# Linear attention, two layer norms and a gated MLP on 8 cores: the output projection in one sweep over eight PSUM banks, and the next tile's attention steps moved

## The reference

```python
qkv = x @ w_qkv; q, k, v = split(qkv, 3)          # 16 heads of 64
q, k = elu(q) + 1, elu(k) + 1
kv = k * v
run_*[t] = d * run_*[t-1] + (kv or k)[t]          # two decays d per head: f and s
out_f = q * run_kv_f / max(sum(q * run_ks_f), 1e-6)   # the same for s
x1 = layernorm(x + concat(out_f, out_s) @ w_out)  # w_out: 2048 x 1024
h  = silu(x1 @ wg.T / 127) * (x1 @ wu.T / 127)    # 3072 wide
y  = layernorm(x1 + h @ wd.T / 127)
```

## Time and profile before

| what | value |
|---|---|
| median of 2 runs | 2699.64 us (2673.45 and 2725.84) |
| profiled execution, device time | 2680.23 us |
| its span, slowest core (core 1) | 2678.6 us; the eight cores 2644.9 to 2678.6 |
| mean granted TensorE clock, core 1 | 0.861 of full speed |
| TensorE busy | 66% of the span |
| VectorE, ScalarE, GpSimd busy | 31%, 20%, 14% |
| chain that ended last | PE 48%, DVE 14%, ACT 13%, DMA 7% |

### The profile page before, as it was taken

How to read it: one execution, slowest core, us unless ns; L and a number is a source line. 1 busy time by engine, 2 the same in 40 slices (tenths; PEclk the granted TensorE clock), 3 DMA queues, 4 the chain that set the end, 5 groups by cost and what they waited for, 6 DMA issues and landing times.

```text
span 2678.6 us, 21229 instructions; the slowest of 8 cores (2644.9 to 2678.6 us)
## 1 busy us (share of the span) xinstructions
PE 1765.9 (66%) x7298; PEld 731.0 (27%) x7298; DVE 832.5 (31%) x994; ACT 537.6 (20%) x574; POOL 384.5 (14%) x308
## 2 busy tenths in 40 slices
PE   0222236788667875777687865877677865787686
PEld 0000012333223322333233322333233322332232
DVE  0122213342234233433334224333334223433111
ACT  0011101230222212221122113221123123221111
POOL 6411111111011111111012011111112001111000
PEclk9666657999879988999889987998799988998898
DMA  9999996324743256324823265313833254314433
GB/s 118 125 124 124 123 129 166 102 83 95 172 123 103 65 140 173 102 67 95 224 87 114 64 150 152 101 53 111 207 102 99 85 163 130 111 59 130 130 106 114
DMA packets 259467, 316.06 MB, mean 118 GB/s; under 512 B 91171, under 2 KB 173092, under 8 KB 257060
## 3 DMA queue, kind: packets, MB, share of 16 engines
q1 hardware_dynamic: 175396, 235.00, 30.7%
q0 software_dynamic: 7168, 46.15, 13.1%
q10 hardware_dynamic: 76800, 33.57, 6.1%
HBM read 318.80 MB, written 54.53 MB: 139 GB/s over the span
## 4 chain that ended last, share of the span: by engine, by line
PE 48%; DVE 14%; ACT 13%; DMA 7%; issue 6%; another core or an unknown queue 5%; POOL 4%; ACTq 1%; DVEq 0%; SPq 0%; POOLq 0%
PE C_ps L719 11%; PE D_ps L719 9%; PE A_ps L391 7%; DVE runs L529 7%; PE C_ps L603 3%; DMA wo_buf<-wo_s 3%; PE C_ps L771 3%; PE D_ps L771 3%; PE D_ps L603 3%; PE A_ps L771 3%; PE B_ps L771 3%; ACT sgb L729 3%; DVE denc L426 2%; DMA wq_buf<-wq_s 2%
## 5 line engine op out<-in xcount | busy, mean ns | idle before, releaser
L719 PE MATMUL C_ps<-y1T,wg_buf 128*128 128x512 bf16 x1536 | 390.5, 413 | 283.7 <-ACT sgb L729 130.1
L391 PE MATMUL A_ps<-xT,wq_buf 128*128 128x512 bf16 x1024 | 280.5, 436 | 170.0 <-DMA wq_buf<-wq_s 136.2
L551 POOL TENSOR_TENSOR runs<-qb,runs 128x1024 f32<-128x1024 f32 x64 | 148.7, 2344 | 1539.1 <-DVE states_sb L538 1539.1
L719 PE MATMUL D_ps<-y1T,wu_buf 128*128 128x512 bf16 x1536 | 347.1, 379 | 1.4 <-DVE hbuf L736 0.4
L736 DVE TENSOR_TENSOR hbuf<-D_ps,sgb 128x1024 bf16<-128x1024 f32 x96 | 117.6, 1225 | 582.2 <-ACT sgb L729 582.2
L719 PEld LDWEIGHTS C_ps<-y1T,wg_buf 128*128 128x128 bf16 x1536 | 155.4, 104 | 515.4 <-issue 377.1
L603 PE MATMUL C_ps<-wo_buf,concat 128*128 128x512 bf16 x512 | 171.0, 419 | 125.0 <-DVE concat L445 62.0
L729 ACT ACTIVATE sgb<-C_ps,cv_sb 128x1024 bf16<-128x1024 f32 x96 | 107.0, 1114 | 522.2 <-PE D_ps L719 433.5
L391 PEld LDWEIGHTS A_ps<-xT,wq_buf 128*128 128x128 bf16 x1024 | 110.3, 110 | 342.0 <-issue 262.3
L719 PEld LDWEIGHTS D_ps<-y1T,wu_buf 128*128 128x128 bf16 x1536 | 149.4, 98 | 185.5 <-issue 7.0
L420 PE MATMUL B_ps<-denr,bones_sb 128*128 128x512 bf16 x128 | 51.3, 493 | 224.1 <-POOL denr L408 180.9
(11 more groups left out here) (71 smaller groups left out, 1242.3 us busy)
## 6 DMA issues: line engine op xcount, KB each, us to landing
wq_buf<-wq_s SPq DMA_DIRECT2D x192, 256.0 KB, 3.8
wg_buf<-wg_s SPq DMA_DIRECT2D x192, 256.0 KB, 3.0
wu_buf<-wu_s SPq DMA_DIRECT2D x192, 256.0 KB, 4.3
wd_buf<-wd_s SPq DMA_DIRECT2D x384, 128.0 KB, 2.3
wo_buf<-wo_s SPq DMA_DIRECT2D x256, 128.0 KB, 3.2
out<-work ACTq DMA_DIRECT2D x64, 256.0 KB, 6.1
xbf<-x POOLq DMA_DIRECT2D x32, 256.0 KB, 187.2
xbm<-xbf POOLq DMA_DIRECT2D x32, 256.0 KB, 4.6
```

The costliest lines, as they stand in the source:

```text
L391: t.matmul(o, a, b, start=f1, stop=f2),
L551: lambda v, q_=qv, r_=kvpart: v.tensor_tensor(r_.rearrange("p (o t) -> p o t", o=2), q_, r_.rearrange("p (o t) -> p o t", o=2), OP.mult),
L719: t.matmul(o, a, b, start=f1, stop=f2),
```

## The change

1. The output projection runs once over `kt`, with `h2` inside it: 8 matmuls a step, into all four PSUM tensors (`bank = (C_ps, D_ps, A_ps, B_ps)`, one per 128 tokens). Its first matmul waits for A_ps and B_ps too. The 6 slots of `wo_buf` hold 3 steps of two halves. All eight evictions come behind the last matmul, in the order c = 2, 3, 0, 1, so that A_ps and B_ps come free first.
2. LN1 is done in two groups of two 128-token blocks, (2, 3) and then (0, 1): sums, two Squares, Ln, Exp, two normalisations, two transposing DMAs.
3. The pieces of the next front move: S2 and S3 both stand behind LN1 and ahead of gate/up (S3 stood behind step 1); S4 to S8 stand behind steps 1, 3, 5, 7, 9; S9 stands between gate/up and down (it stood behind down). The calls inside down are gone.

```diff
-        for h2 in range(2):
-            pspair = (C_ps, D_ps)
-            for k in range(min(6, NKT)):
-                stream_half(sg, "wo", ..., k, h2, k)
-            for kt in range(NKT):
...
-                    if kt == 0 and c == 0:
-                        w = w + (firstB[0] if h2 == 0
-                                 else [(ch_v, ch_v.n)])
+        firstB = [(ch_v, concat_val)] + [
+            (chof(t), v) for key in ("A", "B", "C", "D") for t, v in gPS[key]]
+        bank = (C_ps, D_ps, A_ps, B_ps)
+        for k in range(3):
+            for h2 in range(2):
+                stream_half(sg, "wo", ..., k, h2, k * 2 + h2)
+        for kt in range(NKT):
+            for h2 in range(2):
+                ridx = (kt * 2 + h2) % 6
                 for c in range(NCH):
...
+                        lambda t, o=bank[c][:, h2 * 512:(h2 + 1) * 512],
...
+            if kt + 3 < NKT:
+                for h2 in range(2):
+                    stream_half(sg, "wo", ..., kt + 3, h2, (kt + 3) * 2 + h2)
+        m_wave = ch_m.n
+        for c in (2, 3, 0, 1):
+            for h2 in range(2):
+                prog.op("vector", ...)      # scalar_tensor_tensor, as before
+            gb[c] = ch_v.n
+        gPS["A"] = [("v", gb[2])]
+        gPS["B"] = [("v", gb[3])]
+        gPS["C"] = [("v", gb[0])]
+        gPS["D"] = [("v", gb[1])]
...
+        if a_next_gen is not None:
+            next(a_next_gen, None)                      # S1
...
+        for grp in ((2, 3), (0, 1)):
+            ...                              # sums, waits=[(ch_v, gb[grp[1]])]
+            for c in grp: ...                # Square, then Ln and Exp of two
+            for c in grp: ...                # normalise, DMA transpose to y1T
         if a_next_gen is not None:
             next(a_next_gen, None)                      # S2
+            next(a_next_gen, None)                      # S3
...
         h_done = h_ready
         g["y1T"] = ch_m.n
+        if a_next_gen is not None:
+            next(a_next_gen, None)                      # S9
...
-            if a_next_gen is not None:
-                next(a_next_gen, None)
         g["h"] = ch_m.n
```

More of the change, by code:

```diff
@@ L573, in emit_BCD @@
         concat_val = g["concat_ready"]
[L575 to L578, removed]
+        firstB = [(ch_v, concat_val)] + [
+            (chof(t), v) for key in ("A", "B", "C", "D") for t, v in gPS[key]]
+        bank = (C_ps, D_ps, A_ps, B_ps)
         def lhs_wout(kt, c):
             return concat[:, kt * ST + c * 128: kt * ST + (c + 1) * 128]
-        for h2 in range(2):
-            pspair = (C_ps, D_ps)
-            for k in range(min(6, NKT)):
+        for k in range(3):
+            for h2 in range(2):
                 stream_half(sg, "wo", wo_buf, wo_s, wo_in, wo_slot_g,
-                            wo_cval, k, h2, k)
-            for kt in range(NKT):
-                ridx = kt % 6
+                            wo_cval, k, h2, k * 2 + h2)
+        for kt in range(NKT):
+            for h2 in range(2):
+                ridx = (kt * 2 + h2) % 6
                 for c in range(NCH):
-                    ps = pspair[c // 2]
-                    half = (c % 2)
                     w = [wo_cval[(kt, h2)]]
-                    if kt == 0 and c == 0:
-                        w = w + (firstB[0] if h2 == 0
-                                 else [(ch_v, ch_v.n)])
+                    if kt == 0 and h2 == 0 and c == 0:
+                        w = w + firstB
                     prog.op(
                         "tensor",
-                        lambda t, o=ps[:, half * 512:(half + 1) * 512],
+                        lambda t, o=bank[c][:, h2 * 512:(h2 + 1) * 512],
                         a=lhs_wout(kt, c),
@@ L606, in emit_BCD @@
                 wo_slot_g[ridx] = ch_m.n
-                if kt + 6 < NKT:
+            if kt + 3 < NKT:
+                for h2 in range(2):
                     stream_half(sg, "wo", wo_buf, wo_s, wo_in, wo_slot_g,
[L609 to L614, removed]
+                                wo_cval, kt + 3, h2, (kt + 3) * 2 + h2)
+        m_wave = ch_m.n
+        gb = {}
+        for c in (2, 3, 0, 1):
+            for h2 in range(2):
+                prog.op(
                     "vector",
@@ L617, in emit_BCD @@
                                          c * DM + h2 * 512 + 512],
-                    p_=ps[:, half * 512:(half + 1) * 512],
+                    p_=bank[c][:, h2 * 512:(h2 + 1) * 512],
                     xx=xbm[:, c * DM + h2 * 512: c * DM + h2 * 512 + 512],
@@ L625, in emit_BCD @@
                     inc=ch_v)
-                r1_half[c][h2] = v_r1
-            if a_next_gen is not None and h2 == 1:
-                g["xbm_v"] = ch_v.n
-                next(a_next_gen, None)
-        gPS["C"] = [("v", ch_v.n)]
-        gPS["D"] = [("v", ch_v.n)]
+            gb[c] = ch_v.n
[3 more added lines that the diff above has]
+        gPS["D"] = [("v", gb[1])]
         g["concat"] = ch_m.n
         g["xbm_v"] = ch_v.n
+        if a_next_gen is not None:
+            next(a_next_gen, None)
@@ L635, in emit_BCD @@
         sview = stat[:, so_:so_ + 8].rearrange("p (c u) -> p c u", u=2)
[L636 to L688, removed]
+        for grp in ((2, 3), (0, 1)):
+            c0g = grp[0]
+            v_s1b = prog.op(
+                "vector",
+                lambda v, d=stat[:, so_ + 8 + c0g:so_ + 10 + c0g],
+                a=sview[:, c0g:c0g + 2, 0], b=sview[:, c0g:c0g + 2, 1]:
+                    v.tensor_tensor(d, a, b, OP.add),
+                waits=[(ch_v, gb[grp[1]])], inc=ch_v)
+            v_nmb = prog.op(
+                "vector",
+                lambda v, d=stat[:, so_ + 8 + c0g:so_ + 10 + c0g]:
+                    v.tensor_scalar(d, d, -1.0 / DM, None, OP.mult),
+                waits=[(ch_v, v_s1b)], inc=ch_v)
+            sq_last = None
+            for c in grp:
+                sq_last = prog.op(
+                    "scalar",
+                    lambda s_, z=work[wl][:, c * DM:(c + 1) * DM],
+                    b=stat[:, so_ + 8 + c:so_ + 9 + c],
+                    a_=stat[:, so_ + 12 + c:so_ + 13 + c]:
+                        s_.activation(ebuf[:], z, AF.Square, bias=b,
+                                      accum_out=a_),
+                    waits=[(ch_v, v_nmb), (ch_v, g["eb_r"]),
+                           (ch_s, g["eb_s"])],
+                    inc=ch_s)
+                g["eb_s"] = sq_last
+            v_lnv = prog.op(
+                "scalar",
+                lambda s_, d=stat[:, so_ + 16 + c0g:so_ + 18 + c0g],
+                z=stat[:, so_ + 12 + c0g:so_ + 14 + c0g]: s_.activation(
+                    d, z, AF.Ln, bias=cvap("eps_ln"), scale=cvap("inv_dm")),
+                waits=[(ch_s, sq_last)], inc=ch_s)
+            v_rst = prog.op(
+                "scalar",
+                lambda s_, d=stat[:, so_ + 16 + c0g:so_ + 18 + c0g]:
+                    s_.activation(d, d, AF.Exp, scale=cvap("neghalf")),
+                waits=[(ch_s, v_lnv)], inc=ch_s)
+            for c in grp:
+                v_y1 = prog.op(
+                    "vector",
+                    lambda v, o=y1b[:, c * DM:(c + 1) * DM],
+                    z=work[wl][:, c * DM:(c + 1) * DM],
+                    nm=stat[:, so_ + 8 + c:so_ + 9 + c],
+                    rs=stat[:, so_ + 16 + c:so_ + 17 + c]:
+                        v.tensor_scalar(o, z, nm, rs, OP.add, OP.mult),
+                    waits=[(ch_s, v_rst), (ch_yt, g["xbm_yt"])],
+                    inc=ch_v)
+                g_stat[wl] = ch_v.n
+                dview = y1T.ap().rearrange("p (j t) -> p j t", j=NJ)[
+                    :, :, c * 128:(c + 1) * 128]
+                sview2 = y1b[:, c * DM:(c + 1) * DM].rearrange(
+                    "p (j f) -> p j f", j=NJ)
+                prog.op("scalar",
+                        lambda s_, d=dview, z=sview2: s_.dma_start(
+                            out=d, in_=z, transpose=True),
+                        waits=[(ch_v, v_y1), (ch_m, g["y1T"])],
+                        inc=ch_yt, inc_n=16)
```

## The result

The changed kernel takes 2740.7 us (median of 11 runs) against 2673.3 for the kernel before (10 runs). The ratio is 1.0248 with a 95% interval of 1.0216 to 1.028: 2.5% slower, where +19 us, a change too small to tell, was forecast. The profiled execution takes 2736.2 us (before 2680.2), its span on the slowest core 2734.6. Some executions of every kernel ran with one or both dies at a lower clock (up to 2968 us here); the medians of the two kernels include them, the ratios and the profiles do not.

What follows compares the result with a forecast made beforehand. TensorE's matmuls and the gaps between them (TensorE works 66% of the span) bound the kernel. Seven tiles at +7.7 (+54), the projection -40 and the last tile +5 made 2680.2 + 19 = 2699 us, 8-in-10 range 2656 to 2744.

Steps and rivals of the forecast that it cites:

- S3: Denominator of pair 0 and QKV of pair 1, moved ahead of gate/up where nothing covers it: plus 15.6 us a tile.
- S9: Denominator of pair 3, moved ahead of down: plus 3.4 us there, up to 4.5; minus 12.3 before the projection.
- The serial chain through LN1, the scans and POOL: Idle PE between QKV of pair 0 and the ones-matmuls of S3, which start at 33.1 us.
- The block behind it: Two ones-pairs and QKV of pair 1 in S3: 16.6 us in the new place, without a table load.
- The wait for `wg_buf`: Before gate: its loads stand behind the `wq` loads of S3 in SP's queue, a gap of 4.5 us.
- the sweep: Output projection in one pass, without the pause and one clock restart: minus 5 us a tile, between minus 9 and minus 1.
- With about four in hand PE waits 3.6 us: In the projection, 12 loads land in 17.3 us where 20 are wanted, so PE waits 3.6 us.
- the sweep gains only 1: Rival: what is queued at the DMA engines just shifts and `xT` ends the wait for QKV; 2738 us, chance 0.13.
- its wait for `xT`: Part of that rival: QKV of pair 0 waits for the `xT` transposes, plus 1 us more than taken.
- QKV's wait: Start of QKV of pair 0 waits for A_ps to be evicted, 2.1 us where it waited 1.2: plus 1.
- LN1 of the last tile: Bare LN1 without a next front: eight evictions ahead (2.4 us) and the split's transposes (about 2.5), plus 5 once.
- The clock rival: Rival: all 48 matmuls of QKV of pair 1 stay at 1.2 GHz; +56, 2755 us, chance 0.05.

Runs made afterwards that it cites:

- late stores: Changed kernel with the stores of `out` issued by SP in gate/up of the next tile: 2721.1 us in the profiled execution, no ratio.
- early `xT`: Kernel before with S9 ahead of down and stores in the next gate/up, plus transposes of `xT` issued a tile earlier, ahead of down: ratio 0.9672.

## Why the prediction was right or wrong

**S3: the mechanism right, two ends short.** The serial chain through LN1, the scans and POOL was forecast at 33.1 us and is 33.3; 20.17 of it stood in the start-up. The two groups of LN1 were forecast to lengthen it by 3.1: 33.3 against 30.2 without. The block behind it took 17.4 (forecast 16.6). The wait for `wg_buf` took 6.5 (forecast 4.5; the terms given for it, 50.6 + 0.9 + 3.0, make 54.5 and not 54.2): I took the median landing of a single load from the page, while here twelve loads of gate/up, in six pairs, follow right behind the last of QKV, and gate needs both loads of the first pair. Together with the steps the term is +21.1 instead of +19.0.

**S9: right.** The gap between down and the projection fell by 12.2 (forecast 12.3), and down starts 3.7 later behind the last step (forecast 3.4). What I had only as an upper bound (4.5 with a slower start of down) was passed: down starts at the lower clock (its first pairs of matmuls take 1.06 us, later ones 0.59 with their overlap) and takes 1.3 more, which makes 5.0. In tiles 1 to 6 about 8 matmuls of down stand 0.43 us apart instead of 0.216, where the kernel before has about 2. And the 2.8 us ahead of the projection, which I took as given, are the sweep's own price: with S9 alone they are gone.

**The sweep: the step that failed.** "With about four in hand PE waits 3.6 us" and so minus 5. In the kernel with the sweep alone the projection is 0.6 shorter, in the changed kernel 2.3, and the tile of the sweep alone is not shorter at all. The share of the DMA engines above 1 was the right row, and the reading that the pause was mostly `wo_buf` and not the evictions was right (18 waits of 31.4 us in all against 3 of 9.2); the size was not. My sum had the kernel before waiting 5.8 us and the new one 3.6, as if running through the pause let loads land that had been late. But the 3.6 came from the window of the kernel before, with loads five uses ahead as in both kernels. The same working gives 3.6 for the kernel before too, whose trace has one pause of 5.76 in that window alone, so it was no ground for a gain.

Measured over tiles 1 to 6, the waits inside the projection are 5.9 us before, 5.8 with the sweep alone and 5.1 in the changed kernel. Matmuls at the lower clock, which stand 0.43 us apart instead of 0.216, cost 3.7, 2.8 and 1.8 us. So the sweep alone wins 0.9 of the time at the lower clock, loses part of that again in more and shorter waits, each with some 0.16 us beyond its idle time until matmuls follow at full pace, and then pays 0.8 at QKV for A_ps. In the changed kernel the first matmuls of the projection start at the full clock too, as only 2.8 us of idle time stand ahead of them and not 15.0; in half of the tiles the clock still falls a few matmuls later. In tile 0 and the last tile the changed kernel's projection did save 7.0 and 5.7, so of the 40 us put down for eight tiles 26 came. The late stores show that the stores are the larger part of the waits for `wo_buf`, and the early `xT` that the transposes are the rest. The rival "the sweep gains only 1" gave 2738 us, close to the 2741 measured, and that is partly luck: its wait for `xT` did not come (QKV waited 1.7 for A_ps), and what it left out at S9, down and `wg_buf` filled its place.

**The other terms.** QKV's wait: +0.8, forecast +1. LN1 of the last tile: 22.4 us instead of 17.89, forecast +5; alone, the evictions of the sweep make 2.6 of it and the split 2.1. The clock rival did not come: QKV of pair 1 is back at full clock after its first 16 matmuls. The table loads of the denominator fell to 21.

**The sum.** Per tile the forecast was +2.7 and the measurement +8.7. The 6.0 between them are 2.7 from the sweep, 2.1 from S3 and S9, 1.3 from down and 0.1 from rounding, less 0.2 at QKV. The sweep was inside the bounds I had written down; S9 with down passed its 4.5 and the wait for `wg_buf` its 6. The large ones all lay on the same side, and the sum was a difference of +19.0 and -16.3 taken seven times. The 2741 us lie inside the range of 2656 to 2744, at its upper end; what failed is "no change". So "within 2%" at 0.74 was too sure: 2% was less than 8 us a tile, and my own bounds of the sweep alone spanned as much.

## What to carry to other kernels

Work moved to cover a gap covers it only if its own inputs are ready there: follow the inputs back through every queue, as here DVE behind ACT behind PE. The same move can pay in one place (S9 ahead of down, 2.6%) and cost in another (S3 ahead of gate/up, 3.7%), so price and try each move by itself. A pause at which loads arrive late is not won by removing the synchronisation there; what pays is moving the other transfers out of that stretch, to a place where nothing waits for what they slow down: the stores paid in gate/up, the transposes of `xT` ahead of down did not.

## What the runs showed of the hardware

Issuing a transposing DMA is not a fixed price to the engine that issues it: the first two of LN1 take ACT 2.65 us in every tile of the changed kernel, and 5.3 to 6.5 in seven tiles when nothing but the place of the gate/up loads is changed, so that twelve loads of 256 KB are issued just before; a single one took up to 4.9. In the last tile of that kernel it is 2.6 again. Everything behind them on ACT waits. Why the issue takes longer is not shown. Two executions of the same projection in different tiles differ by more than 5 us (34.6 to 40.2 with the sweep alone); an effect of 1 us a tile in a stretch limited by DMA needs many tiles to be seen.
